# Routed rows that carry x with half of x1: the experts add it and scatter to the final place

## The chip, the core and the metric

The program runs on one core of a Trainium2 chip. The metric is the device time of one execution in microseconds, as the median of three runs: 1472.13 us before the change (1472.07 to 1477.34). Line numbers, as L1299, are those of the kernel before.

## What is computed

The input x has 4096 tokens of 128 numbers. Three blocks follow one another, each added to a running x:

```python
x = x + 0.5 * ffn(layernorm(x))       # first ffn
x = x + attn(layernorm(x))            # RWKV-6 recurrence
x = x + 0.5 * ffn(layernorm(x))       # second ffn, same weights

def ffn(z):
    x1 = z + msa(layernorm(z))        # softmax attention, 16 heads of 8, 512 tokens per batch
    return x1 + moe(layernorm(x1))    # one of 8 experts per token: gelu(h @ w1[e]) @ w2[e]
```

So each ffn block ends in x + 0.5 x1 + 0.5 y, where y is what the token's expert gives.

## The kernel before

The program is a chain of phases with a barrier of all engines between them: load_constants, mixer, expert, turn, recurrence, mixer, expert, combine. Each phase writes one instruction list per engine. The order on an engine is that of the code, and waits are on semaphores.

**Start.** In the first block SP issues 4 loads of constants, 8 slices of x (256 KB each) and 8 tables for the routing, and all engines wait for its end at a barrier (L259 to L282).

**Mixer.** It computes x1 in 8 batches b of 4 head groups g. Q and K are split in a high and a low part (`parts`: the high part by ScalarE, L866, the low part by VectorE, L979, or GpSimd, L518), and stored by SP to DRAM (`store`, L445), one image of 512 KB each per batch. From there SP loads each head group into stacked tiles `q_stack` and `k_stack` (`load_group`): 12 DMAs a group, 4 of 64 KB for q (L458) and 8 of 32 KB for k (L461), because both hold copies of the parts in several rows. TensorE makes scores (L652), VectorE their maxima (L986), TensorE the exponents' arguments (L660), ScalarE the exponentials (L933), TensorE the values (L670). `BEFORE`, `jobs` and `AFTER` are written lists that place the other work between these. Before the loop VectorE sets four stripes of `k_stack` to one (L1094) and then makes the low parts of batches 0 and 1. `halve` (L1022) makes x + 0.5 x1 in x_all, `norm_rows` (L1049) the normed x1 in `rows`, whose column 128 is the token's number. GpSimd scatters each row to its expert's place in the DRAM tensor `sorted` by indirect DMA (L558), 4 per batch. At the end SP writes 8 blocks of padding rows, one after each expert's rows, at places it reads from `pad_row` (L495, L496), and waits for them. GpSimd waits for all scatters.

**Expert.** 40 slots of 128 rows, as a software pipeline over three steps. In step j, SP has loaded tile j of `sorted` in one of 4 buffers `xt` (L1205), TensorE transposes it (L1228), ScalarE scales it (L1257), VectorE copies the expert's w1 (L1276); in step j+1 TensorE does the first layer (L1234), ScalarE the gelu (L1262); in step j+2 TensorE does the second layer (L1241), VectorE copies the result to `yt` (L1281). GpSimd casts the token numbers of a tile in the step after its transpose (L1295) and then scatters the rows of the tile before it to `expert_out` by indirect DMA (L1299). SP loads the next tile into a buffer once TensorE has transposed it and GpSimd has cast its numbers; the steps run in a loop unrolled by 4.

**Turn and combine.** The turn phase loads `expert_out` in 8 slices, VectorE adds half of it to x_all (L1400), norms it, TensorE transposes it for the recurrence. The combine phase at the end of the program loads it in 8 slices (L1317), adds half of it to x_all (L1323) and stores the output from ScalarE's queue (L1330).

**Phase exit.** All engines drain, GpSimd clears the phase's semaphores, and a barrier follows (L65, L66).

Of the kernel before, what the change touches and what calls it, by code (L numbers as in the profile page):

```python
# [5 lines left out]
F32 = mybir.dt.float32  # L6
# [7 lines left out]
P = 128  # L14
# [178 lines left out]
def load_constants(nc, ctx, d, x_all, padding, xs):  # L193
# [46 lines left out]

    def load_late(sp, part):
# [17 lines left out]
    with nc.Block() as block:  # L259
        @block.sync  # L260
        def _(sp):
            for dst, src in first:
                sp.dma_start(dst[:], src).then_inc(loaded, 16)
            for j in range(SL):
                here = slice(j * ST, (j + 1) * ST)
                sp.dma_start(x_all[:, here, :], x_slices[:, here, :]).then_inc(s["x_loaded"][j], 16)
            for dst, src in routing:
                sp.dma_start(dst[:], src).then_inc(s["routing_loaded"], 16)
# [10 lines left out]
        def _(pool):  # L279
            nc.gpsimd.memset(s["B_lora"][:], 0.0).then_inc(zeros_set, 1)  # L280
            nc.gpsimd.memset(padding[:, :, 0:P], 0.0).then_inc(zeros_set, 1)
            nc.gpsimd.memset(padding[:, :, P:], float(TOK)).then_inc(zeros_set, 1)  # L282
    return s, load_late, wait_rest


# [12 lines left out]
def mixer_phase(nc, ps, s, x_all, z_all, rows, expert, first_row, xs, qd, kd, load=None):  # L298
    with Phase(nc) as ctx:
# [71 lines left out]
        scattered, padded = sem("scattered"), sem("padded")  # L371
# [5 lines left out]
        PER_LOAD = 16 * 12  # L377
# [62 lines left out]
        with nc.Block() as block:  # L440
            @block.sync
            def _(sp):
                def store(j, k, dram):
                    sp.wait_ge(low[k], j + 1)
                    sp.dma_start(dram.rearrange("(c i) h t -> (i h) c t", i=DK)[:, :, j * SW:(j + 1) * SW],  # L445
                                 parts[k][:].bitcast(F32)).then_inc(stored[k], 16)

                def load_group(b, g):
                    def heads_of(dram, first, count, e):
                        heads = dram.rearrange("c (n p e) t -> c n p e t", p=PAIRS, e=2)  # L450
                        return heads[first:first + count, g, :, e, b * T:(b + 1) * T]

                    sp.wait_ge(stored["q"], 16 * (b + 1))
                    sp.wait_ge(stored["k"], 16 * (b + 1))
# [1618 lines left out]
```

## Time and profile before

The profile is of one execution that took 1473.18 us, of which 1471.4 us are the span from the first to the last instruction.

| what | us |
|---|---|
| median of the runs | 1472.13 |
| profiled execution | 1473.18 |
| its span | 1471.4 |
| first exponential of the first mixer | at 58.24 |
| first mixer to the start of the first expert phase | to 493.21 |
| first expert phase | 493.21 to 584.8 |
| turn phase | 585.3 to 610.2 |
| second mixer to the start of the second expert phase | 883.2 to 1362.74 |
| second expert phase | 1362.74 to 1453.5 |
| combine phase and end | 1453.5 to 1471.4 |

Starts are counted from the first instruction. The next phase begins only once the slowest engine has drained, so the end of a phase is set by the one wait that ends last there, and busy shares over the whole span say little about it.

### The profile page before, as it was taken

To read this page: it belongs to the slowest core of one execution; us is meant where nothing else is said; L and a number is where in the kernel's file an instruction comes from. 1 tells how busy PE (TensorE), PEld (TensorE's weight loads), DVE (VectorE), ACT (ScalarE), POOL (GpSimd) and SP (SyncE) were. 2 spreads that over 40 slices of the span, in tenths; PEclk is the share of its full clock that TensorE was granted. 3 is DMA by queue.
4 is the path that set the end of the run, shared out by engine and by line. 5 is a ranking of instruction groups with operands and counts; after the bars stand their busy time and mean duration, and the time that the engine had idled before them with its cause. 6 is when DMAs were issued, how large, how long until landed. Compare 5 with 4: busy or idle time off the path is not lost. (4 is left out here: it accounts for less than half of the span.)

```text
span 1471.4 us, 36051 instructions
## 1 busy us (share of the span) xinstructions
PE 1230.9 (84%) x12512; PEld 661.3 (45%) x12513; DVE 1042.9 (71%) x1842; ACT 860.7 (58%) x1742; POOL 553.6 (38%) x797
## 2 busy tenths in 40 slices
PE   2799999999997596398888754999999999993893
PEld 1234444444443596145455442344444444442893
DVE  3889988988992332478788745888898988963232
ACT  2288877778775353444334411588788778881451
POOL 6122324323212354355676536222332431222462
PEclk9599999999999799599999955799999999996896
DMA  4322442222110121100000003122122122100224
GB/s 117 71 74 74 130 121 68 82 71 73 55 36 9 53 67 47 42 2 3 3 2 2 3 1 87 57 75 65 49 82 73 53 81 66 56 15 30 56 66 122
DMA packets 81540, 82.40 MB, mean 56 GB/s; under 512 B 16249, under 2 KB 53724, under 8 KB 81392
## 3 DMA queue, kind: packets, MB, share of 16 engines
q1 hardware_dynamic: 72560, 69.88, 16.7%
q0 software_dynamic: 4608, 8.44, 1.8%
q10 hardware_dynamic: 4224, 2.10, 0.5%
q8 instruction: 94, 1.54, 0.4%
q14 instruction: 54, 0.44, 0.1%
HBM read 50.42 MB, written 29.93 MB: 55 GB/s over the span
## 5 line engine op out<-in xcount | busy, mean ns | idle before, releaser
L986 DVE TENSOR_REDUCE maxima<-ps 128x2 f32<-128x1024 f32 x512 | 616.2, 1222 | 89.8 <-PE ps L652 88.5
L933 ACT ACTIVATE probs<-ps 128x512 f32<-128x512 f32 x1024 | 550.8, 600 | 120.3 <-PE ps L660 109.7
L652 PE MATMUL ps<-k_stack,q_stack 62*128 62x512 f32 x1024 | 390.0, 473 | 39.0 <-DVE maxima L986 21.7
L660 PE MATMUL ps<-q_stack,k_stack 64*128 64x512 f32 x1024 | 396.3, 464 | 4.2 <-ACT q_whole L869 3.4
L670 PE MATMUL ps<-probs,v_stack 128*32 128x256 f32 x4096 | 329.6, 394 | 0.9 <-ACT probs L933 0.4
L652 PEld LDWEIGHTS ps<-k_stack,q_stack 62*128 62x128 f32 x1024 | 160.1, 194 | 235.9 <-issue 138.3
L660 PEld LDWEIGHTS ps<-q_stack,k_stack 64*128 64x128 f32 x1024 | 159.2, 187 | 30.5 <-ACT q_whole L869 8.6
L670 PEld LDWEIGHTS ps<-probs,v_stack 128*32 128x32 f32 x4096 | 81.7, 108 | 166.6 <-issue 148.3
L532 POOL CAST neg_wide<-maxima 128x16 fp32r<-128x16 f32 x64 | 12.6, 196 | 286.7 <-DVE maxima L986 286.7
L1299 POOL DMA_INDIRECT expert_out<-yt,number x80 | 78.3, 979 | 72.4 <-POOL number L1295 44.1
L1276 DVE COPY w_now<-w 128x512 f32 x80 | 34.6, 433 | 80.1 <-issue 42.2
L1234 PE MATMUL ps<-xT,w_now 128*128 128x128 f32 x640 | 89.7, 285 | 0.2
L1241 PE MATMUL ps<-w,hidT 128*128 x640 | 84.7, 276 | 0.0
L1234 PEld LDWEIGHTS ps<-xT,w_now 128*128 128x128 f32 x640 | 80.9, 198 | 3.0 <-issue 2.4
L1257 ACT ACTIVATE xT<-ps,ln_b,ln_w 128x128 f32<-128x128 f32 x80 | 36.6, 457 | 73.1 <-PE ps L1228 73.1
L1241 PEld LDWEIGHTS ps<-w,hidT 128*128 128x128 f32 x640 | 78.2, 193 | 0.1
L558 POOL DMA_INDIRECT sorted<-rows,slot x64 | 63.6, 994 | 37.8 <-issue 20.8
L542 POOL TENSOR_TENSOR rows<-o_rows,inv 128x128 f32<-128x128 f32 x64 | 30.8, 501 | 122.1 <-DVE inv L993 122.1
L1262 ACT ACTIVATE hidT<-ps 128x512 f32<-128x512 f32 x80 | 47.8, 597 | 40.3 <-PE ps L1234 39.8
L1731 POOL TENSOR_TENSOR r_kx<-r_kx,r_k_factor 128x512 f32<-128x512 f32 x48 | 61.6, 1284 | 9.8 <-PE ps L1909 6.4
L1712 POOL TENSOR_TENSOR r_mixed<-r_shift,zT 128x512 f32<-128x512 f32 x40 | 58.7, 1474 | 16.0 <-DVE r_shift L1588 16.0
L1281 DVE COPY yt<-ps 128x128 f32<-128x128 f32 x80 | 23.3, 291 | 48.8 <-PE ps L1241 48.1
(208 smaller groups left out, 1622.7 us busy)
## 6 DMA issues: line engine op xcount, KB each, us to landing
q_stack<-q_split SPq DMA_DIRECT2D x256, 64.0 KB
k_stack<-k_split SPq DMA_DIRECT2D x512, 32.0 KB
q_split<-q_parts SPq DMA_DIRECT2D x16, 512.0 KB, 2.7
k_split<-k_parts SPq DMA_DIRECT2D x16, 512.0 KB, 3.6
xt<-sorted SPq DMA_DIRECT2D x80, 64.5 KB
w<-in_L_ffn_w SPq DMA_DIRECT2D x16, 256.0 KB, 3.0
rows<-expert_out SPq DMA_DIRECT2D x16, 256.0 KB, 4.5
x_all<-in_L_attn_x SPq DMA_DIRECT2D x8, 256.0 KB, 5.1
```

The source lines that it names most:

```text
L558: pool.indirect_dma_start(xs, bass.IndirectOffsetOnAxis(ap=slot[:, i:i + 1], axis=0), rows[:, i, :], None).then_inc(scattered, 16)
L652: mm = t.matmul(psS[:, h, :], qs[g][score_rows(h), h // 2, u * P:(u + 1) * P], ks[g][score_rows(h), h // 2, :], start=True, stop=True)
L660: t.matmul(ring("e", G, u, n), ks[G % NG][half(h), h // 2, u * P:(u + 1) * P], qs[G % NG][half(h), h // 2, :], start=True, stop=True).then ...
L670: last = t.matmul(psO[VW * h:VW * (h + 1), here], vs[g][:, u, h, :], probs[u % 2][:, h, here], start=(g % SHARE == 0 and u == 0 and part = ...
L933: a.activation(probs[u % 2][:, h, :], ring("e", G, u, n), ACT.Exp, scale=float(DK) ** -0.5).then_inc(e_read, 1)
L986: v.tensor_reduce(maxima[G % 2][:, :, pair, u:u + 1], psS[:, 2 * pair:2 * pair + 2, :], AX_X, ALU.max, negate=True).then_inc(s_read, 1)
L1234: last = t.matmul(psH[o][:, c * P:(c + 1) * P], w1_now[o][:, c * P:(c + 1) * P], xT[o][:], start=True, stop=True)
L1241: last = t.matmul(psY[i][:, 0:P], hidT[i][:, c, :], s["w2"][:, ds(second_expert, 1), c, :], start=(c == 0), stop=(c == HC - 1))
L1262: a.activation(hidT[o][:].rearrange("p c t -> p (c t)"), psH[o], ACT.Gelu_apprx_tanh).then_inc(hidT_kept, 1)
L1299: pool.indirect_dma_start(ys, bass.IndirectOffsetOnAxis(ap=number[out_slot][:], axis=0), yt[out_slot][:], None, bounds_check=TOK - 1, oob_ ...
L1712: g.tensor_tensor(mixed[f][:], shift[f % 2][:], x, ALU.add).then_inc(mixed_ready.sem, 1)
L1731: g.tensor_tensor(dst[:].rearrange("p (k m) -> p k m", m=m), src[:].rearrange("p (k m) -> p k m", m=m), k_factor[l][:].rearrange("p n two ...
```

## The change

- `rows` becomes 257 numbers wide: normed x1, x_all, token number. x_all is now the middle part of `rows`, so a scattered row is 1028 bytes where it was 516. `sorted`, `padding` and `xt` are as wide.
- In the expert phase GpSimd copies the middle part of `xt` to a new tile `before` ahead of the cast of the numbers, SP's reload waits for it too, and VectorE's copy to `yt` becomes 0.5 y + `before`. The scatter goes to `after_experts` in the first ffn, and to the output in the second.
- The turn phase loads x_all itself and adds nothing. The combine phase goes.
- The first block loads 2 slices of x; the other 6 and the routing tables are issued by SP at the start of the mixer's block.
- The DRAM images of q and k have 32 rows, each part twice; each store is 2 DMAs of 512 KB, and a head group is loaded by 4 DMAs of 128 KB.
- VectorE makes the low parts of batch 0 ahead of the four memsets.
- Four padding blocks are written from SP's queue, four from ScalarE's.

```diff
@@ load_constants
+    def load_early(sp):
+        for j in range(2, SL):
+            here = slice(j * ST, (j + 1) * ST)
+            sp.dma_start(x_all[:, here, :], x_slices[:, here, :]).then_inc(s["x_loaded"][j], 16)
+        for dst, src in routing:
+            sp.dma_start(dst[:], src).then_inc(s["routing_loaded"], 16)
...
-            for j in range(SL):
+            for j in range(2):
                 here = slice(j * ST, (j + 1) * ST)
                 sp.dma_start(x_all[:, here, :], x_slices[:, here, :]).then_inc(s["x_loaded"][j], 16)
-            for dst, src in routing:
-                sp.dma_start(dst[:], src).then_inc(s["routing_loaded"], 16)
@@ mixer_phase
+                def store_k(j):
+                    sp.wait_ge(low["k"], j + 1)
+                    for a in range(SPLITS):
+                        every_other = kd.rearrange("(c a i) h t -> a c i h t", c=SPLITS, a=SPLITS)[a, :, :, :, j * SW:(j + 1) * SW]
+                        sp.dma_start(every_other.rearrange("c i h t -> (i h) c t"),
+                                     parts["k"][:].bitcast(F32)).then_inc(stored["k"], 16)
...
                     for e in range(2):
-                        for a in range(SPLITS):
-                            row = HALF * e + a * SPLITS * DK
-                            sp.dma_start(qs[g][row:row + SPLITS * DK, :, :].bitcast(F32),
-                                         heads_of(qd, 0, SPLITS * DK, e)).then_inc(loaded[g], 16)
-                            for at in (row, row + DK):
-                                sp.dma_start(ks[g][at:at + DK, :, :].bitcast(F32),
-                                             heads_of(kd, a * DK, DK, e)).then_inc(loaded[g], 16)
+                        here = slice(HALF * e, HALF * e + ROWS)
+                        sp.dma_start(qs[g][here, :, :].bitcast(F32), heads_of(qd, e)).then_inc(loaded[g], 16)
+                        sp.dma_start(ks[g][here, :, :].bitcast(F32), heads_of(kd, e)).then_inc(loaded[g], 16)
...
-                for e in range(E):
+                for e in range(E // 2):
                     row = sp.value_load(pad_row[0:1, e:e + 1], min_val=0, max_val=E * (TOK + P) - P)
                     sp.dma_start(xs[ds(row, P), :], s["padding"][:, 0, :]).then_inc(padded, 16)
...
+                act.wait_ge(pads_ready, 1)
+                for e in range(E // 2, E):
+                    row = act.value_load(pad_row[0:1, e:e + 1], min_val=0, max_val=E * (TOK + P) - P)
+                    act.dma_start(xs[ds(row, P), :], s["padding"][:, 0, :]).then_inc(act_padded, 16)
+                act.wait_ge(act_padded, 16 * (E - E // 2))
...
+                for k in "qk":
+                    low_part(0, k)
                 for i in range(2):
                     for e in range(2):
                         v.memset(ks[i][HALF * e + ROWS:HALF * e + STACK, :, :].bitcast(F32), 1.0).then_inc(k_set, 1)
-                for j in range(2):
-                    for k in "qk":
-                        low_part(j, k)
+                for k in "qk":
+                    low_part(1, k)
@@ expert_phase
                         sp.wait_ge(x_turned, RING * (turn - 1) + i + 1)
+                        sp.wait_ge(carried, RING * (turn - 1) + i + 1)
                         sp.wait_ge(numbered, RING * (turn - 1) + i + 1)
...
-                        v.tensor_copy(yt[out_slot][:], psY[i][:, 0:P]).then_inc(y_kept, 1)
+                        after(vec, carried, j, 2)
+                        v.scalar_tensor_tensor(yt[out_slot][:], psY[i][:, 0:P], 0.5, before[out_slot][:], ALU.mult,
+                                               ALU.add).then_inc(y_kept, 1)
...
-                        nc.gpsimd.tensor_copy(number[at][:], xt[at][:, P:]).then_inc(numbered, 1)
+                        nc.gpsimd.tensor_copy(before[at][:], xt[at][:, P:2 * P]).then_inc(carried, 1)
+                        nc.gpsimd.tensor_copy(number[at][:], xt[at][:, 2 * P:]).then_inc(numbered, 1)
@@ program
-        x_all, z_all = sb("x_all", [P, NT, P]), sb("z_all", [P, NT, P])
-        rows = sb("rows", [P, NT, P + 1])
+        z_all, rows = sb("z_all", [P, NT, P]), sb("rows", [P, NT, 2 * P + 1])
+        x_all = rows[:, :, P:2 * P]
...
-        ffn()
-        combine_phase(nc, x_all, y_all, ys, out)
+        ffn(out.rearrange("b t c -> (b t) c"))
```

## Rows read from the trace of the kernel before

**Rows 1.** The page of the profile: span, and busy time of each engine.
```profile
span 1471.4 us, 36051 instructions
...
PE 1230.9 (84%) x12512; PEld 661.3 (45%) x12513; DVE 1042.9 (71%) x1842; ACT 860.7 (58%) x1742; POOL 553.6 (38%) x797
```

**Rows 2.** Timeline of 0 to 14 us: start, length, engine, line, instruction [idle before].
```profile
2.58 5.73 SPq L266 DMA_DIRECT2D x_all<-in_L_attn_x  x8
...
13.01 0.87 DVE L950 BATCH_NORM_STATS2 stats<-x_all 128x6 f32<-128x128 f32 x4 [8.19 <-PEq L259]
```

**Rows 3.** Source view of line 266: from issue to landing.
```profile
DMA to landing us min/median/max: 3.1/5.1/5.9
```

**Rows 4.** Timeline of the second mixer's start, 893 to 908 us.
```profile
893.97 0.59 ACT L869 ACTIVATE k_whole<-ps 128x512 f32<-128x512 f32 x1
...
895.90 0.69 DVE L979 TENSOR_TENSOR k_parts<-k_whole,k_parts 128x512 fp32r<-128x512 f32 x1
...
900.64 0.33 SPq L458 DMA_DIRECT2D q_stack<-q_split  x1
...
907.30 1.22 PE L652 MATMUL ps<-k_stack,q_stack 62*128 62x512 f32 x4 [7.58 <-DMA k_stack<-k_split]
```

**Rows 5.** DMA view of 891 to 900 us in 40 equal slices.
```profile
GB/s 0 0 0 0 0 0 0 0 0 0 0 0 0 0 0 0 0 0 0 0 0 0 0 0 0 0 309 382 419 391 410 391 401 410 419 400 382 310 9 27
```

**Rows 6.** Timeline of the first mixer's end, 481 to 492 us.
```profile
481.32 8.46 SPq L496 DMA_DIRECT2D sorted<-padding  x8
...
484.83 0.96 POOL L558 DMA_INDIRECT sorted<-rows,slot  x1 [0.30 <-issue]
```

**Rows 7.** Source view of line 66 (phase exit) in windows at 491, 584, 1453 us.
```profile
L66 SPq DRAIN  x1: 7/7/7, 491.6 to 491.6; - x1
...
L66 SPq DRAIN  x1: 7/7/7, 584.8 to 584.8; - x1
...
L66 SPq DRAIN  x1: 7/7/7, 1453.5 to 1453.5; - x1
```

**Rows 8.** Timeline inside the first expert phase.
```profile
512.38 0.63 DVE L1276 COPY w_now<-w 128x512 f32 x1 [1.48 <-PE ps L1234]
...
512.75 0.29 POOL L1295 CAST number<-xt 128x1 int32<-128x1 f32 x1
...
540.88 0.29 DVE L1281 COPY yt<-ps 128x128 f32<-128x128 f32 x1 [0.62 <-PE ps L1241]
...
541.13 0.20 POOL L1295 CAST number<-xt 128x1 int32<-128x1 f32 x1
...
541.73 0.43 DVE L1276 COPY w_now<-w 128x512 f32 x1 [0.56 <-issue]
...
542.05 0.97 POOL L1299 DMA_INDIRECT expert_out<-yt,number  x1 [0.72 <-POOL number L1295]
...
544.51 0.14 PEld L1228 LDWEIGHTS ps<-ident,xt 128*128 128x128 f32 x1
...
577.55 0.97 POOL L1299 DMA_INDIRECT expert_out<-yt,number  x1 [0.61 <-issue]
```

**Rows 9.** Source views of lines 1205 (541.9 to 543.8 us) and 1299 (500 to 580 us).
```profile
L1205 SPq DMA_DIRECT2D xt<-sorted x1: 338/338/338, 542.3 to 542.3; - x1
...
L1299 POOL DMA_INDIRECT expert_out<-yt,number x40: 974/974/1154, 502.2 to 578.8; - x40
```

**Rows 10.** DMA issues on the page: KB each, median us from issue to landing.
```profile
w_qkv<-in_w_qkv SPq DMA_DIRECT2D x1, 192.0 KB, 2.3
...
ident<-in_ident SPq DMA_DIRECT2D x1, 64.0 KB, 1.9
```

**Rows 11.** Groups of instructions on POOL: count | busy us, mean ns | idle before.
```profile
L512 POOL TENSOR_SCALAR z_all<-x_all,moments,scales 128x128 f32<-128x128 f32 x64 | 50.5, 796 | 0.4
...
L524 POOL COPY v_stack<-v_all 128x144 f32<-128x144 f32 x64 | 20.0, 318 | 57.3 <-PE ps L670 57.0
```

**Rows 12.** Timeline of the turn phase, first add.
```profile
588.20 0.69 DVE L1400 SCALAR_TENSOR_TENSOR x_all<-rows,x_all 128x512 f32<-128x512 f32 x1 [10.49 <-DMA rows<-expert_out]
```

More of the change, by code:

```diff
@@ new lines, in store_q @@
+                def store_q(j):
+                    sp.wait_ge(low["q"], j + 1)
+                    for a in range(SPLITS):
+                        half_rows = qd[a * SPLITS * DK:(a + 1) * SPLITS * DK, :, j * SW:(j + 1) * SW]
+                        sp.dma_start(half_rows.rearrange("(c i) h t -> (i h) c t", i=DK),
+                                     parts["q"][:].bitcast(F32)).then_inc(stored["q"], 16)
+                def store_k(j):
+                    sp.wait_ge(low["k"], j + 1)
+                    for a in range(SPLITS):
+                        every_other = kd.rearrange("(c a i) h t -> a c i h t", c=SPLITS, a=SPLITS)[a, :, :, :, j * SW:(j + 1) * SW]
+                        sp.dma_start(every_other.rearrange("c i h t -> (i h) c t"),
+                                     parts["k"][:].bitcast(F32)).then_inc(stored["k"], 16)
@@ L469, in place @@
                                      max_rows[G % 2][e * count:(e + 1) * count, :].bitcast(F32)).then_inc(rows_placed, 16)
-                store(0, "q", qd)
-                store(0, "k", kd)
+                if load is not None:
+                    load[0](sp)
+                store_q(0)
+                store_k(0)
                 for g in range(NG):
                     load_group(0, g)
-                store(1, "q", qd)
-                store(1, "k", kd)
+                store_q(1)
+                store_k(1)
                 place(0)
@@ L482, in _ @@
                     if g == 3 and b + 2 < B:
[L483 to L484 removed]
+                        store_q(b + 2)
+                        store_k(b + 2)
                     if b + 1 < B:
@@ L555, in scatter @@
                     pool.wait_ge(row_ready, p + 1)
+                    pool.wait_ge(halved, p + 1)
                     pool.wait_ge(placed, p + 1)
@@ L894, in number @@
                     act.wait_ge(s["routing_loaded"], s["routing_count"])
-                    a.activation(rows[:, :, P:], s["token"][:].unsqueeze(2), ACT.Copy).then_inc(numbered, 1)
+                    a.activation(rows[:, :, 2 * P:], s["token"][:].unsqueeze(2), ACT.Copy).then_inc(numbered, 1)
                 def job(kind, j):
@@ L1195, in expert_phase @@
         number = [ctx.enter_context(nc.sbuf_tensor(own(nc, f"number{i}"), [P, 1], I32)) for i in range(RING)]
-        passed, numbered = sem("passed"), sem("numbered")
+        before = [ctx.enter_context(nc.sbuf_tensor(own(nc, f"before{i}"), [P, P], F32)) for i in range(RING)]
+        passed, numbered, carried = sem("passed"), sem("numbered"), sem("carried")
         second_done, y_kept, y_stored = sem("second_done"), sem("y_kept"), [sem(f"y_stored{i}") for i in range(RING)]
@@ L1304, in _ @@
                     pool.wait_ge(y_stored[i], 16 * (SLOTS // RING))
-def combine_phase(nc, x_all, y_all, ys, out):
-    with Phase(nc) as ctx:
-        y_loaded = [ctx.semaphore(f"y_loaded{j}") for j in range(SL)]
-        added, stored = ctx.semaphore("added"), ctx.semaphore("stored")
-        slices = [slice(j * ST, (j + 1) * ST) for j in range(SL)]
-        with nc.Block() as block:
-            @block.sync
-            def _(sp):
-                for j, here in enumerate(slices):
-                    sp.dma_start(y_all[:, here, :], tiles_of(ys)[:, here, :]).then_inc(y_loaded[j], 16)
-            @block.vector
-            def _(vec):
-                for j, here in enumerate(slices):
-                    vec.wait_ge(y_loaded[j], 16)
-                    nc.vector.scalar_tensor_tensor(x_all[:, here, :], y_all[:, here, :], 0.5, x_all[:, here, :],
-                                                   ALU.mult, ALU.add).then_inc(added, 1)
-            @block.scalar
-            def _(act):
-                for j, here in enumerate(slices):
-                    act.wait_ge(added, j + 1)
-                    act.dma_start(slices_of(out)[:, here, :], x_all[:, here, :]).then_inc(stored, 16)
-                act.wait_ge(stored, 16 * SL)
 class Signal:
@@ L1378, in turn_phase @@
         rstd, shift, normed = sbs("r_rstd", [P, ST]), sbs("r_shift", [P, ST]), sbs("r_normed", [P, ST, P])
-        y_loaded = [sem(f"y_loaded{j}") for j in range(SL)]
-        added, stats_made, moments_made, var_ready = sem("added"), sem("r_stats_made"), sem("r_moments_made"), sem("r_var_ready")
+        x_loaded = [sem(f"x_loaded{j}") for j in range(SL)]
+        stats_made, moments_made, var_ready = sem("r_stats_made"), sem("r_moments_made"), sem("r_var_ready")
         constants, rstd_ready, shift_ready = sem("r_constants"), sem("r_rstd_ready"), sem("r_shift_ready")
```

67 lines of the change are left out of this document (26 added, 41 removed).

## The prediction

> **What bounds the kernel now.** I read the page first. No engine is busy over the whole span [rows 1], so the stages have different limits, and the change touches their seams and the expert phases, hardly the attention in between. So I read the timelines at the seams, then one turn of the expert loop.
>
> Start: the first instruction that works on x, the statistics at 13.01, does not wait for its slice but for a block in which SP issues x for 5.73 us from 2.58, and the tables after it; VectorE, which had waited there for the four loads of constants, had been idle for 8.19 us [rows 2]. A mixer's start then hangs on q and k: low part of k, store, load, first scores at 907.30 with PE idle for 7.58 us on the load [rows 4]. A mixer's end hangs on SP: 8 padding blocks issue for 8.46 us from 481.32 while GpSimd has finished its scatters at 485.79 [rows 6], and SP drains at 491.6 [rows 7]. In the expert loop, PE paces: `yt` is followed 0.88 us later by the scatter (541.17 to 542.05), also where the number cast ended well before (577.55) [rows 8], so GpSimd waits for the result, not the result for GpSimd. The end is the combine phase, from the drain at 1453.5 to 1471.4 [rows 1, 7].
>
> **The change, part by part.** Span of the profiled execution 1471.4, its time 1473.18; the median is 1.05 below that time, and I take the same off at the end.
>
> *Later loads of x.* Two slices issue in 2 of 8 parts of 5.73 us, so SP is through at 4.0, VectorE at 13.01 - 8.19 = 4.8, and the barrier falls near 5. Slice 0 lands 3.1 us after its issue at best [rows 3], at 5.7. The statistics start at 5.7 instead of 13.01: **-7.3** (bounds: -8.0 if only the barrier counts, -5.3 with the median landing of 5.1). What SP issues now in the mixer's block is the rest, some 8.5 us, done by 14; the first low part comes at 25.1 - 7.3 = 18 or earlier, so it is not late. Slices 2 to 7 are used after 50 us. The wider padding memset ends before 4 us on GpSimd and is hidden.
>
> *Low parts ahead of the memsets.* k is whole at 894.56 and its low part ran only at 895.90, ending at 896.59 [rows 4]. It can now end at 895.3, 1.3 earlier, and q's about 1.7 before it. The memsets (about 4.7 us) end at 900 and the scores come after that, so nothing is late through them.
>
> *Images twice.* Before, 1 MB went out at some 400 GB/s in 2.6 us [rows 5], and SP began to load 4.05 us after the low part's end (900.64). Now 2 MB go out. q's megabyte goes first, k's starts when q's is out, at 897.2, and ends at 899.8; with the same tail the load begins at 900.6 to 900.9. The doubled store thus eats the 1.3 us. The load of the first group then issues 4 DMAs for 12. Before, 12 took about 4.2 us and the scores came 2.5 us after the last. Now 4 take 1.6, and 512 KB have to arrive in 4 DMAs instead of trickling: I take 904.8 for the first score, **-2.5** (bounds: 0 if the transfer and not the issue was the limit, -3.6 if neither the store nor the size costs anything). Twice, once per mixer: **-5.0**. Inside a mixer loads come a head group ahead of their use; I cost them and the extra 0.5 MB stores at nothing. If that cover failed, PE would show waits on `k_stack` DMAs outside the two starts; now it has them only there.
>
> *Padding on two queues.* Four blocks on SP end 4.2 us sooner, near 487.4. But then GpSimd is last: it ends its scatters at 485.79, and the landing of a last scatter can be read only at an expert phase's end, 578.8 + 0.97 to the drain at 584.8 [rows 7, 9], 5.0 us. So the drain falls at 490.8 instead of 491.6: **-0.8**, twice **-1.6** (bounds -3.6 each if a scatter lands in 2.2 us, as small plain DMAs do [rows 10]; +0.5 if the doubled row makes it later). The added wait on `halved` is met before `row_ready` in every batch, for halve stands before norm_rows; nobody queues behind it.
>
> *Expert phases.* GpSimd gains a copy of 128x128 per slot. The nearest row is the copy of 128x144 with 0.318 us, the farthest a tensor_scalar of 128x128 with 0.796 [rows 11]; same operation, so 0.30. The slot is (578.8 - 502.2)/39 = 1.96 us [rows 9]. GpSimd needs 0.97 + 0.20 + 0.30 and a gap between number and scatter, at most 0.61 where it was not the wait for `yt` alone [rows 8]: at most 2.08, likely 1.8. So it does not bind by itself. What binds is the ring of four `xt` buffers. The cast of tile j ends at 541.33, SP's reload of that buffer issues at 542.3 [rows 9], lands 1.9 later (64 KB [rows 10]) at 544.2 to 544.3, and PE wants it at 544.51 [rows 8]. Slack 0.2 us. The change adds 0.30 for the copy, 0.05 for the longer `yt` instruction (an estimate: one more operand), and 0.2 for 131 KB instead of 66 (192 KB land 0.4 later than 64 KB [rows 10], for twice this growth): 0.55 a turn of four slots. PE thus stalls 0.35 a turn, ten turns: 3.5 us a phase, **+7.0** (bounds 0 if the copy takes 0.15; see rivals for the top). The carried wait of SP is met before the numbered one; VectorE has slack of over a microsecond in a slot.
>
> One rule bears on this. By the Trainium skill, page SBUF — State Buffer, section "Who interferes with whom", VectorE in a two-port mode (copies between SBUF tiles can be in one) and GpSimd hold a shared port pair in turn, the later one blocked fully. The trace agrees where the two meet: a w1 copy of 0.63 over a cast of 0.29 at 512.38, where at 541 they are apart with 0.43 and 0.20 [rows 8].
>
> *Turn phase.* The first add of 0.69 goes [rows 12]; after it ScalarE paces the slices, so only this first one counts: **-0.7** (bounds 0 and -2).
>
> *No combine.* The last scatter goes straight to the output, with the same wait and drain at 1453.5. After that only the outer exit remains, about 1 us. 1471.4 - 1454.5 = **-16.9** (bounds -16 and -17.4).
>
> Sum: -7.3 - 5.0 - 1.6 + 7.0 - 0.7 - 16.9 = -24.5. 1473.2 - 24.5 = 1448.7, and on the level of the median **1448 us**.
>
> **The rivals.**
> - *GpSimd becomes the bound of the slot.* For: the gap after a cast is 0.72 at 542.05 [rows 8]. If it is needed in full, the slot is 0.97 + 0.20 + 0.30 + 0.72 = 2.19, +0.23 for 39 slots = 9 us a phase instead of 3.5: 1459. Against: the gap of 0.61 at 577.55.
> - *The copy meets the w1 copy.* Then it is late by up to 0.43 every turn, 4.3 us a phase more: 1456.5. Against: at 541.73 the w1 copy starts 0.4 us after the cast has ended, more than the 0.30 of the new copy [rows 8]. The skill's rule (the same page) would make this price the full one whenever they meet.
> - *Scatters land early.* Then the padding was the whole limit and each mixer ends 3.6 earlier, not 0.8: 1442. By the Trainium skill, page DMA: Bandwidth & Descriptors, section "Latency and other measured facts", a DMA's fixed cost is about 2 us, which would put it there. The 5.0 us at the expert's end speaks against it.
> - *Smaller ones.* Loading q and k is limited by the transfer: +5, 1453. A 1028-byte row costs GpSimd twice the time per scatter: four at each mixer end, +3.9 twice, 1456.
> - *Slower.* The GpSimd copy costs what the tensor_scalar costs and the gap of 0.72 stays. The slot becomes 0.97 + 0.20 + 0.80 + 0.72 = 2.69, +0.73 for 78 slots = +57 for +7: 1498. All else gives 31.5 back, 0.40 a slot, so it decides from a copy of about 0.47 us on. For: 0.796 is the same shape on the same engine. Against: it computes, the copy row does not.
>
> **How the numbers follow.** Forecast 0.50, GpSimd bound 0.14, port 0.08, early scatters 0.12, the smaller two 0.12, slower 0.04. The predicted time is the first's, 1448. The range takes in the early scatters with a ring that costs nothing (about 1437) and GpSimd as bound with a smaller start (about 1461). A measurement here tells 0.5%, 7.4 us, from no change; every case but the last is below 1464.8. Faster 0.93, same 0.03, slower 0.04.
>
> **What would show it.** Statistics at about 5.7; first score some 10 us earlier than before in the first mixer and 2.5 in the second; the first expert phase's slot at about 2.05 with PE waiting for `xt` once a turn, and GpSimd idle before the scatter for less than before; the drain of the mixer set by the last scatter, 5 us after its end; nothing after the last scatter but 6 us. Wrong would be: a slot that is GpSimd from end to end, PE waits on `k_stack` inside a mixer, a scatter on GpSimd over 1 us, or a w1 copy and the new copy always side by side.

## The result and the profile after

The kernel after takes 1458.91 us (median of 4 runs, 1456.21 to 1460.41), the kernel before 1473.35 beside it on the same chip: a ratio of 0.989, interval 0.9869 to 0.9911 (the two medians alone would give 0.990). By the medians that is 14.4 us faster, by the interval 13 to 19. The median lies inside the predicted range of 1437 to 1461, but 10.9 us above the predicted 1448. The profiled execution took 1458.89 us, with a span of 1456.9.

The page of the profile after, the lines that answer to [rows 1]:

```profile
span 1456.9 us, 35636 instructions
...
PE 1232.6 (85%) x12512; PEld 662.6 (45%) x12513; DVE 1033.9 (71%) x1826; ACT 860.6 (59%) x1742; POOL 573.1 (39%) x877
```

The totals say little, as before: PE is busy for 1.7 us more, GpSimd for 20, and the span is 14.5 us shorter. So I put the same moments of the two traces side by side. They are read from timelines and source views: first score, last cast of `slot` (the last thing before the last four scatters), and the moment at which the engines leave each phase's block.

| moment, us | before | after | the stretch before it changed by |
|---|---|---|---|
| first statistics | 13.0 | 5.6 | -7.4 |
| first score, mixer 1 | 37.2 | 27.0 | -2.8 |
| last `slot` cast, mixer 1 | 480.0 | 469.7 | -0.1 |
| mixer 1 left | 491.6 | 484.1 | **+2.8** |
| expert phase 1 left | 584.7 | 579.0 | +1.8 |
| turn phase left | 610.1 | 603.3 | -1.1 |
| statistics, mixer 2 (behind the recurrence) | 883.3 | 875.7 | -0.8 |
| first score, mixer 2 | 907.3 | 898.8 | -0.9 |
| last `slot` cast, mixer 2 | 1349.5 | 1343.4 | **+2.4** |
| mixer 2 left | 1361.1 | 1359.2 | **+4.2** |
| expert phase 2 left | 1453.4 | 1455.8 | +4.3 |
| end of the span | 1471.4 | 1456.9 | -16.9 |

The start, in the timeline of 0 to 8 us of the kernel after. VectorE waits 0.71 us for its slice of x where it had waited 8.19 for the block [rows 2]:

```profile
5.59 0.87 DVE L968 BATCH_NORM_STATS2 stats<-rows 128x6 f32<-128x128 f32 x4 [0.71 <-DMA rows<-in_L_attn_x]
```

The end, in the source view of line 66, 1450 to 1460 us. Two drains within 0.5 us, and then the span is over, where the combine phase stood before [rows 7]:

```profile
L66 SPq DRAIN  x2: 7/7/7, 1455.9 to 1456.4; - x2
```

**A mixer's end.** This is the seam that went the other way than predicted. First the source view of the block's line, 479 to 493 us, kernel before (an engine's COMPARE_BRANCH stands behind its last wait, its DRAIN behind that; the EVENT_SEMAPHORE is where all leave):

```profile
L440 POOLq COMPARE_BRANCH  x1: 43/43/43, 487.8 to 487.8; - x1
L440 POOLq DRAIN  x1: 2686/2686/2686, 488.0 to 488.0; - x1
L440 SPq COMPARE_BRANCH  x1: 43/43/43, 491.2 to 491.2; - x1
...
L440 SPq EVENT_SEMAPHORE  x1: 17/17/17, 491.6 to 491.6; - x1
```

And the same view of the kernel after, 475 to 486 us:

```profile
L446 ACTq COMPARE_BRANCH  x1: 43/43/43, 480.4 to 480.4; - x1
...
L446 POOLq COMPARE_BRANCH  x1: 43/43/43, 481.1 to 481.1; - x1
L446 POOLq DRAIN  x1: 2686/2686/2686, 481.3 to 481.3; - x1
L446 SPq COMPARE_BRANCH  x1: 43/43/43, 481.4 to 481.4; - x1
...
L446 SPq EVENT_SEMAPHORE  x1: 17/17/17, 484.1 to 484.1; - x1
```

(A landing is counted here from the end of the last scatter instruction on GpSimd to the moment at which the engine that waits for it passes its wait; a drain is the time of the DRAIN instruction behind that.) Before, GpSimd is through its wait for the scatters at 487.8, 2.0 us behind its last scatter (end 485.79), drains for 2.69 us and is ready at 490.7; SP's padding is through at 491.2 and decides, by half a microsecond. After, SP is through at 481.4, but GpSimd passes its wait at 481.1, 5.6 us behind its last scatter (end 475.52), and its drain then runs with nothing beside it: 484.0. In mixer 2 it is 7.0 us (1349.20 to 1356.2). So the scatters land late and GpSimd's drain is added to that. The DMA view of 478 to 494 us, kernel before (KB each, median us from issue to landing):

```profile
sorted<-padding SPq DMA_DIRECT2D x8, 64.5 KB, 2.0
```

and of 468 to 484 us, kernel after:

```profile
sorted<-padding ACTq DMA_DIRECT2D x4, 128.5 KB, 5.0
sorted<-padding SPq DMA_DIRECT2D x4, 128.5 KB, 5.4
```

Eight transfers on one queue, issued one in 1.06 us (8.46/8, [rows 6]), landed in 2.0 us each. Twice the bytes on two queues, beside four scatters of twice the bytes, land in 5.0 to 5.4.

**The expert phase.** The groups of PE and GpSimd in the kernel after, 1368 to 1450 us (count | busy us, mean ns | idle before):

```profile
L1249 PE MATMUL ps<-ident,xt 128*128 128x128 f32 x37 | 10.6, 285 | 3.3 <-DMA xt<-sorted 3.2
...
L1323 POOL DMA_INDIRECT out<-yt,number x40 | 39.2, 980 | 30.4 <-DVE yt L1303 17.8 <-issue 11.7 <-POOL number L1319 0.9
L1318 POOL COPY before<-xt 128x128 f32<-128x128 f32 x38 | 11.8, 311 | 0.0
```

The slot went from 1.96 us [rows 9] to (573.15 - 494.9)/39 = 2.01 in phase 1 and, from (1447.6 - 1372.2)/39 = 1.93 to (1450.0 - 1371.1)/39 = 2.02, in phase 2. PE, which had waited for no `xt` in this stretch, now waits 3.2 us for its loads. The copy costs 0.31 us, the scatter 0.98, as before. VectorE's `yt` now waits for the copy in some turns, 3.1 us in all in this window.

### The profile page after: what moved, and what is told of

It reads as the page before. It is cut to its first block and busy times, and to the rows that moved or that the text cites. A ratio compares the mean times of both kernels' runs of the same rounds, so it can differ in the third digit from the quotient of the medians.

```text
span 1456.9 us, 35636 instructions
## 1 busy us (share of the span) xinstructions
PE 1232.6 (85%) x12512; PEld 662.6 (45%) x12513; DVE 1033.9 (71%) x1826; ACT 860.6 (59%) x1742; POOL 573.1 (39%) x877
## 5 line engine op out<-in xcount | busy, mean ns | idle before, releaser
L544 POOL CAST neg_wide<-maxima 128x16 fp32r<-128x16 f32 x64 | 12.6, 196 | 283.0 <-DVE maxima L1004 283.0
L1303 DVE SCALAR_TENSOR_TENSOR yt<-ps,before 128x128 f32<-128x128 f32 x80 | 23.3, 291 | 57.2 <-PE ps L1262 50.6
L1249 PE MATMUL ps<-ident,xt 128*128 128x128 f32 x80 | 23.9, 298 | 46.7 <-DMA xt<-sorted 46.2
```

## The experiments

The times of whole kernels are medians of several runs, except where one run is named; moments inside a kernel are from its one trace. The runs were taken in four groups, each on a chip of its own with the kernel before beside it: 1472.91 us for `pads_one`, `before_pads_two`, `pads_after` and `ring8`; 1473.12 for the parts one at a time; 1472.23 for `sp_waits`, `best` and `best_two`; 1474.71 for `best_once`. What a kernel gains is therefore told against the before of its own group; the kernel after gained 14.4. The ratios' intervals are 1.5 to 7 us wide to either side, so a difference of 3 us between two changed kernels is settled by the traces, if at all, and not by the medians.

### Padding: one queue or two, beside the scatters or behind them

`pads_one`: the kernel after with all padding on SP again.

```diff
-                for e in range(E // 2):
+                for e in range(E):
...
-                act.wait_ge(pads_ready, 1)
-                for e in range(E // 2, E):
...
```

Expected:

> The changed kernel with all eight padding blocks back on SP's queue; everything else as changed. In the changed kernel the mixer ends 14.5 and 15.9 us after the last slot cast (before the change 11.6 and 11.7), and the last scatter lands 8.7 us after its end on GpSimd, with the DMA engines full for 8 us. Theory 'crowding': the eight padding blocks of 131 KB now leave in 4 us beside the scatters, and the last scatter waits in the crowd. Then with the blocks spread over 8.5 us the drain comes 11.6 to 12.5 us after the slot cast, and the kernel gains 4 to 6 us: about 1454. Rival 'long rows': a scatter of 1028-byte rows lands late by itself; the drain stays at 14.5 to 16 us and the time at 1459.

Measured: 1455.31 us, ratio 0.9871 (0.9848 to 0.9894), 17.6 us below its before, 3.2 more than the kernel after gained, with intervals that overlap. SP is through at 481.9 instead of 481.4, later; but GpSimd passes its wait at 479.7, 4.65 us behind its last scatter instead of 5.6, and the block is left 13.5 and 14.9 us behind the last cast instead of 14.4 and 15.8. That lies between the two theories: crowding had 11.6 to 12.5, long rows 14.5 to 16. The ends hold 1.8 of the 3.2 us, and in mixer 2 the end is again SP's padding (through at 1357.0, with GpSimd drained at 1355.2). The 8.7 us that the expectation called the landing is the landing and the drain together.

`before_pads_two`: the kernel before, only with the padding on two queues. Expected:

> The kernel before with only one part of the change: four padding blocks from SP's queue and four from ScalarE's, rows of 516 bytes. My forecast for this part was -0.8 us a mixer, since the last scatter would land 5.0 us after its end and set the drain: drain 10.8 us after the slot cast, time 1.6 us less. 'Crowding' with half the bytes: between that and no change (11.6). If scatters land in about 2 us when nothing is beside them, the drain comes 8 us after the slot cast and the time is 7 us less.

Measured: 1476.51 us, ratio 1.0025 (1.001 to 1.004): slower, where the prediction had taken 1.6 us off. The source view of the block's line, 479 to 494 us:

```profile
L440 ACTq COMPARE_BRANCH  x1: 38/38/38, 488.9 to 488.9; - x1
L440 SPq COMPARE_BRANCH  x1: 43/43/43, 489.1 to 489.1; - x1
...
L440 POOLq COMPARE_BRANCH  x1: 43/43/43, 489.3 to 489.3; - x1
L440 POOLq DRAIN  x1: 2686/2686/2686, 489.5 to 489.5; - x1
...
L440 SPq EVENT_SEMAPHORE  x1: 17/17/17, 492.3 to 492.3; - x1
```

The padding is done 2.1 us sooner than before, as meant (489.1 for 491.2). The scatters are through at 489.3 instead of 487.8, though their last one ended at the same moment (485.84 for 485.79), and with the 2.69 us of drain behind them the block is left at 492.3 instead of 491.6. With the short rows the second queue thus costs the scatters 1.5 us. Each mixer's end is 0.7 us longer, 1.4 together; of the 3.1 us by which this trace's span is longer, 2.2 lie inside mixer 2, in a stretch that is taken up in the section on the prediction.

`pads_after`: the kernel after, both padding queues waiting for all scatters first (one run).

```diff
                 sp.wait_ge(pads_ready, 1)
+                sp.wait_ge(scattered, 16 * NT)
...
                 act.wait_ge(pads_ready, 1)
+                act.wait_ge(scattered, 16 * NT)
```

Expected:

> The changed kernel with both queues of padding waiting until all scatters have landed; the time is not the point, the issue of the first padding block is, since it shows when the last scatter lands with nothing beside it. 'Crowding': first block issues 5.0 to 5.5 us after the last scatter's end, as at an expert phase's end. 'Long rows': 8 us or more after it. Time about 1465 in both.

Measured: 1461.06 us in its one run. GpSimd passes its wait 1.7 us behind its last scatter (475.27 to 477.0): without the padding beside them, even the 1028-byte rows land as fast as the short ones did beside 64 KB blocks. In mixer 2 it is 2.3. Both theories had more, 5.0 and 8. So a scatter's own landing is about 2 us, and the 5.0 us that the prediction had read at the expert phase's end is a landing and a drain. The trace of the kernel before has the two apart, in the source view of the expert block's line, 560 to 590 us: the last scatter ends at 579.8, GpSimd is through its wait 1.3 us later and then drains for 3.33.

```profile
L1200 POOLq COMPARE_BRANCH  x1: 38/38/38, 581.1 to 581.1; - x1
L1200 POOLq DRAIN  x1: 3325/3325/3325, 581.2 to 581.2; - x1
```

### GpSimd's drain

`sp_waits`: the kernel after, only with the waits for the last scatters on SP instead of GpSimd, in both phases.

```diff
                 sp.wait_ge(padded, 16 * (E // 2))
+                sp.wait_ge(scattered, 16 * NT)
...
                 scatter(B - 1)
-                pool.wait_ge(scattered, 16 * NT)
...
                         load(RING * turn + i, i)
+                for i in range(RING):
+                    sp.wait_ge(y_stored[i], 16 * (SLOTS // RING))
...
                 pipeline(pool, SLOTS, 2, step, unroll=RING)
-                for i in range(RING):
-                    pool.wait_ge(y_stored[i], 16 * (SLOTS // RING))
```

Expected:

> The kernel after, only with the waits for the last scatters moved from GpSimd to SyncE, in the mixer and in the expert phase. In the traces GpSimd's DRAIN at the end of a mixer takes 2.69 us in every kernel and 3.3 us at the end of the expert phase, and starts only when its wait for the scatters is over; all engines leave the phase when it ends. Theory: this drain in sequence sets the end; with the wait elsewhere it runs while the scatters and the padding land. Mixer end: 484.1 becomes about 481.8, the expert phase ends about 3 us earlier; 2 * 2.3 + 2 * 3 = 10 us, a median of about 1449. Rival: the drain's duration is the landing of the DMAs that GpSimd issued, so that it grows by what the wait no longer covers, and nothing is gained (1457 to 1460).

Measured: 1449.75 us, ratio 0.9828 (0.9785 to 0.9871): 22.5 us below its before, 8.0 more than the kernel after gained. The source view of the block's line, 468 to 483 us:

```profile
L446 POOLq DRAIN  x1: 10546/10546/10546, 471.1 to 471.1; - x1
...
L446 ACTq COMPARE_BRANCH  x1: 43/43/43, 479.7 to 479.7; - x1
...
L446 SPq COMPARE_BRANCH  x1: 41/41/41, 480.4 to 480.4; - x1
```

and of the expert block's line, 568 to 577 us:

```profile
L1220 POOLq DRAIN  x1: 4788/4788/4788, 571.0 to 571.0; - x1
```

Both theories had a part. The drain does run beside the landing now, but it is no fixed 2.69 us: it grew to 10.5 us and ends at 481.7, 1.3 us behind SP's last wait; in the expert phase it went from 3.33 us behind the wait to 4.79 in place of it. These two records start before the last scatters have run: behind the end of the last scatter (474.7 and 572.5) the drain lasts 7.0 and 3.3 us. From the last scatter's end to the leaving of the block: 8.6 and 10.0 us became 7.1 and 7.8 in the mixers, 4.9 became 3.5 in each expert phase. That is 1.5 + 2.2 + 1.4 + 1.4 = 6.5 us by the wait's place, not the 10 I had put down. The other 1.5 lie in stretches that the edit doesn't touch and that differ between executions by as much (the recurrence took 270.8 to 275.7 us in the fourteen traces).

### The ring of the expert phase

`ring8`: the kernel after with eight buffers instead of four.

```diff
-RING = 4
+RING = 8
```

Expected:

> The changed kernel with 8 instead of 4 buffers for xt, yt, before and number (and the step loop unrolled by 8). Theory 'ring': in the changed kernel the reload of a buffer reaches TensorE late once a turn; with eight buffers the waits for xt after the first tiles go, the slot falls from 2.01 and 2.02 us to 1.96 or less, and the kernel gains 3 to 5 us: about 1455. Rival 'GpSimd': its list of copy, cast and scatter paces the slot; the slot stays at 2.0 and the time at 1459.

Measured: 1449.74 us, ratio 0.9837 (0.9805 to 0.987): 23.2 us below its before, 8.7 more than the kernel after gained, and more than was expected. By the traces the ring holds 7.3 of it: the two expert phases are 2.3 and 5.0 us shorter than in the kernel after. Mixer 2 is also shorter, by 2.0 us at its start and 2.1 behind it, and other stretches are longer; the section on the prediction comes back to both. The same groups, 1368 to 1450 us:

```profile
L1249 PE MATMUL ps<-ident,xt 128*128 128x128 f32 x35 | 9.7, 277 | 0.0
...
L1323 POOL DMA_INDIRECT out<-yt,number x39 | 38.4, 985 | 18.8 <-issue 16.3 <-POOL number L1319 1.6 <-DVE yt L1303 1.0
L1318 POOL COPY before<-xt 128x128 f32<-128x128 f32 x38 | 11.8, 311 | 0.0
```

(The window also holds the end of the phase, which this kernel reaches earlier; the rates are in the slots.) PE waits for no load. The slot is 1.92 us in phase 1 and 1.89 in phase 2: below the kernel after by 0.09 and 0.13, and below the kernel before by 0.04 in both. The copy is still there and costs the slot nothing, and `yt` waits for no copy in this window. So four buffers may have been a small limit even before the change (that kernel wasn't run with eight); after it they are one.

### The parts one at a time, added to the kernel before

`before_x_later`, only the later loads of x:

```diff
-            for j in range(SL):
+            for j in range(2):
                 here = slice(j * ST, (j + 1) * ST)
                 sp.dma_start(x_all[:, here, :], x_slices[:, here, :]).then_inc(s["x_loaded"][j], 16)
-            for dst, src in routing:
-                sp.dma_start(dst[:], src).then_inc(s["routing_loaded"], 16)
...
+                if load is not None:
+                    load[0](sp)
```

> The kernel before, only with the later transfers of x and of the routing's constants put behind the first groups' work. The prediction's first term is -7.3 us. The trace after has the first statistics 7.42 us earlier, and if that gain is this part's alone and nothing gives it back, the median is 1472.9 - 7.4 = 1465.5. Rival: part of the gain is given back because x now lands among the stores and loads of the q and k images; then the first scores come less than 7.4 us earlier and the median is above 1467. Second rival: the whole mixer's start is set by something else that also changed, and this part alone gives under 3 us (above 1470).

Measured: 1465.72 us, ratio 0.9952 (0.9934 to 0.997): -7.4, by the interval -4 to -10, as the first theory has it; that it agrees to the tenth is luck. First score at 29.8, last cast at 472.4.

`before_images`, only the q and k images twice, with the changed functions `store_q`, `store_k` and `load_group`:

```diff
-                PER_LOAD = 16 * 12
+                PER_LOAD, STORED = 16 * 4, 16 * SPLITS
...
-                store(0, "q", qd)
-                store(0, "k", kd)
+                store_q(0)
+                store_k(0)
```

> The kernel before, only with the q and k images written twice into memory by the stores and each group's load made of 4 transfers of whole images instead of 12 parts. The order of the low parts stays. If this part is what brought the first scores of mixer 1 earlier by 2.8 us beyond the gain of x, the median falls by 2 to 5 us, to 1468 to 1471, with the first score at about 34.5 us. Rival: the order of the low parts on VectorE did it; then the first score stays at 37 us within 0.7 and the time within 1 us of before, and the next kernel shows the gain.

Measured: 1473.08 us, ratio 0.9995 (0.9981 to 1.001): nothing, as the rival has it. From the statistics to the first score it is 0.4 us less in mixer 1 (23.8) and 1.3 us more in mixer 2 (25.3).

`before_low`, only the order on VectorE:

```diff
+                for k in "qk":
+                    low_part(0, k)
                 for i in range(2):
...
-                for j in range(2):
-                    for k in "qk":
-                        low_part(j, k)
+                for k in "qk":
+                    low_part(1, k)
```

> The kernel before, only with the first low parts of q and k put ahead of VectorE's four memsets of the k images. If the order is what counts, the first score comes 1 us or more earlier in each mixer and the median is 1469 to 1471.5. If the images count, this is within 1 us of before (1472 to 1474) and the first score is at 36.6 to 37.2 us.

Measured: 1468.46 us, ratio 0.9971 (0.9961 to 0.9981): -4.7, a little more than the first theory had. First score 2.4 us earlier in mixer 1 (34.8) and 4.7 in mixer 2 (902.6), of which 2.8 lie between the statistics and the score.

`carry_alone`, only the wide rows, the sum in the expert phase and no last stage (the other parts undone; padding on SP):

> The kernel before, only with the routed rows carrying x and half of x1, the expert phase adding them and scattering to the tokens' rows, and no stage at the end; x early, the images once, the old order of the low parts, padding on one queue. The prediction's terms are +3.5 us per expert phase, -0.7 for the turn and -16.9 for the last stage: 1472.9 - 10.6 = 1462.3, with nothing for the longer rows that the mixer scatters. The rival, from the traces: the longer rows also cost at the end of each mixer, where the kernel after with one padding queue spends 13.6 and 15.0 us after the last slot instead of 11.6 and 11.7: 5.3 us more; with +1.7 and +4.3 us in the expert phases and -1.2 in the turn this makes 1472.9 - 16.9 + 5.3 + 6.0 - 1.2 = 1466.1.

Measured: 1462.95 us, ratio 0.9944 (0.9922 to 0.9965): -10.2 by the medians, -5 to -11.5 by the interval, which holds both the prediction's -10.6 and the rival's -6.8. The trace has the rival's mechanism, at half its price: the expert phases are 3.0 and 4.0 us longer, the turn 1.3 shorter, and the mixers' ends 1.0 and 1.5 longer, where the prediction had nothing. With -16.9 for the last stage that is -8.7; 2.4 us more come from the recurrence, which the edit doesn't touch. So the nearness to -10.6 is luck.

### The best of it

`best`: eight buffers, all padding on SP, SP waits for the scatters. `best_two`: the same, padding on two queues.

> The kernel after with eight buffers for the expert phase's tiles instead of four, all padding on SyncE, and the waits for the scatters on SyncE. Eight buffers alone gave 1449.7. With the padding on one queue SyncE's own 8 transfers land at 481.9, so the mixer's end gains little over one queue alone: 482.7 to 482.3, against 484.1 of the kernel after, 3 us for both mixers; the expert ends gain 3 us each if the drain theory holds: 1449.7 - 3.5 - 6 = 1440. If it doesn't: 1446.

> As the kernel before this one, but with the padding on two queues as in the kernel after. With GpSimd's drain out of the way the end is set by the last landing alone: the padding's last at 481.4 on two queues and 481.9 on one, the scatters at 481.1 and 479.7. So now two queues and one differ by under 1.5 us over both mixers, either way: 1439 to 1441. If two queues stay slower by 3 us as in the kernel after, then it isn't the drain that made them so.

Measured: `best` 1437.68 us (1437.17 to 1440.04), ratio 0.975 (0.9707 to 0.9794), the fastest kernel of this study. It is 34.5 us below its before, 20.1 more than the kernel after gained. `best_two` 1441.98 (1436.91 to 1442.64), ratio 0.9767 (0.972 to 0.9814). Their intervals overlap, and their mixers' ends are alike: 12.5 and 13.6 us behind the last cast with one queue, 12.8 and 13.9 with two. So with the waits on SP the second queue loses 0.3 us an end instead of 0.9, and gained nothing in any of the three arrangements that were tried. The ends are set differently from what was expected: with one queue SP's padding is last (480.9, GpSimd drained at 479.8), with two it is still GpSimd's drain (481.6, SP through at 480.4).

`best_once`: `best`, with the images written once and 12 loads a group.

> The best kernel so far (eight buffers, padding on SyncE alone, SyncE waits for the scatters), with the q and k images written once and loaded in 12 parts a group again, as before the change. The images alone moved nothing when added to the kernel before (1473.08 against 1473.12). Theory: they are worth nothing here either, and this is 1436.5 to 1439. Rival: they pay once VectorE's order of the low parts no longer hides them, since the first score waited for the k image's load again in the kernel after; then this is 1.5 to 4 us slower, 1439.5 to 1442.

Measured: 1442.33 us (1441.26 to 1443.78), ratio 0.9788 (0.9769 to 0.9808), 32.4 us below its before, where `best` was 34.5 below: the images are worth 2.2 us here. The two ratios' intervals overlap, so the runs alone don't settle it; the traces do. From the statistics to the first score it is 22.3 and 22.2 us with one image in the two mixers, 21.2 and 21.1 in `best`: 1.1 each, 2.2 together. So the rival holds, at its lower end: the images pay once the order on VectorE is the new one, though they paid nothing alone. The timeline of mixer 2's start, 862 to 892 us, kernel `best`:

```profile
879.20 0.69 DVE L992 TENSOR_TENSOR k_parts<-k_whole,k_parts 128x512 fp32r<-128x512 f32 x1 [1.01 <-ACT k_whole L882]
...
884.83 0.33 SPq L471 DMA_DIRECT2D q_stack<-q_split  x1
...
888.99 1.22 PE L665 MATMUL ps<-k_stack,q_stack 62*128 62x512 f32 x4 [4.79 <-DMA k_stack<-k_split]
```

and 865 to 897 us, kernel `best_once`:

```profile
882.64 0.69 DVE L988 TENSOR_TENSOR k_parts<-k_whole,k_parts 128x512 fp32r<-128x512 f32 x1 [1.01 <-ACT k_whole L878]
...
886.10 0.33 SPq L464 DMA_DIRECT2D q_stack<-q_split  x1
...
893.46 1.22 PE L661 MATMUL ps<-k_stack,q_stack 62*128 62x512 f32 x4 [5.95 <-DMA k_stack<-k_split]
```

The trade is in the open: from the low part's end to the first load 4.94 us with two images, 2.77 with one; from the first load to the first score 4.16 with two, 7.36 with one. +2.2 and -3.2.

## Why the prediction was right, and where it wasn't

It was right in sign and range. Of the 10.0 us that lie between the forecast for the span, -24.5, and the measured -14.5, one term holds most.

*The mixer's end is the term that failed.* The prediction took the padding on two queues at -0.8 a mixer, with bounds of -3.6 and +0.5; measured, +2.8 and +4.2, in sum 8.6 us off. Its picture was right in one thing, that GpSimd would be last. It failed in "the landing of a last scatter can be read only at an expert phase's end, ... 5.0 us". That 5.0 holds 1.3 us of landing and 3.33 of drain, was read where no padding moves, was taken as a landing alone, and was carried to a place where eight blocks of 128 KB go out at the same time. What the runs showed in its place: a landing of about 2 us without the padding (`pads_after`, 1.7 and 2.3), plus a drain of 2.69 us behind GpSimd's wait. The landing is stretched by the company: to 3.5 by two padding queues with the short rows, to 3.1 and 2.7 by the long rows on one queue (`carry_alone`), to 5.6 and 7.0 by both (after). `pads_one`, the long rows on one queue too, has 4.65 and 4.0: why more than `carry_alone` stays open. The longer rows at a mixer's end, a bound of +0.5 in the prediction, cost 1.0 and 1.5 us in `carry_alone`. The remedy of waiting elsewhere, `sp_waits`, is the test of the drain's part.

By the Trainium skill, page DMA: Bandwidth & Descriptors, section "Latency and other measured facts", a DMA's fixed cost is about 2 us; `pads_after` agrees with 1.7 and 2.3. The prediction had set this rule against the 5.0 of the trace and believed the 5.0 to be the same thing. The rival built on it, "scatters land early" (1442), had the landing right and the result wrong, since it left out both the drain and the company.

*Later loads of x*: -7.3 predicted, -7.4 measured, in the kernel after and alone.

*Low parts and images*: -2.5 a mixer predicted, -2.8 and -0.9 measured. The sum was near, its terms were not. The order on VectorE was put at 1.3 and is worth 2.3 to 2.8 (`before_low`): with q's low part ahead of the memsets, q's store is out before k's begins and k's lands sooner. In the timelines the time from the end of k's low part to the first load falls from 4.05 [rows 4] to 2.8 (893.15 to 895.93). The doubled store costs 2.2, not the 1.3 that was said, and the fewer loads give 3.2. In mixer 2 of the kernel after the load came 2.0 us later still than in `best` or in `ring8`, whose mixers are written alike (894.62 - 887.75 = 6.9 against 4.9). That is a wait for the k images to land. The traces show what it goes with: in this stretch of mixer 2 the DMA view lists one packet of a queue of kind "instruction", 0.02 MB, 0.4% of 16 engines over 15 us, so about 1 us of one engine. The four kernels with this mixer and four buffers (after, `pads_one`, `pads_after`, `sp_waits`) all have that packet and take 23.0 to 23.2 us from the statistics to the first score; the three with this mixer and eight buffers (`ring8`, `best`, `best_two`) don't have it and take 21.1 to 21.2. `before_images`, with 25.3, has it too. In mixer 1 none of them has it, and there the kernel after takes 21.4. So `ring8` owes 2.0 us of its gain to this start and not to the rate of its slots. That the packet causes the wait wasn't tested.

```profile
887.06 0.69 DVE L997 TENSOR_TENSOR k_parts<-k_whole,k_parts 128x512 fp32r<-128x512 f32 x1 [1.01 <-ACT k_whole L882]
...
894.62 0.33 SPq L471 DMA_DIRECT2D q_stack<-q_split  x1
...
898.85 1.22 PE L665 MATMUL ps<-k_stack,q_stack 62*128 62x512 f32 x4 [6.68 <-DMA k_stack<-k_split]
```

(Timeline of the kernel after, 885 to 900 us.) The DMA view of the same window (packets, MB, share of 16 engines):

```profile
q8 instruction: 1, 0.02, 0.4%
```

The loads inside the mixers were rightly put at nothing: between the two starts PE shows no wait for a `k_stack` DMA in the kernel after.

*The expert phases*: +3.5 each predicted, +1.8 and +4.3 measured, +3.0 and +4.0 in `carry_alone`. The mechanism, four buffers whose reload comes late, is shown by PE's waits and by `ring8`. Both rivals on the copy fail: GpSimd waits for `yt` (17.8 us) more than for anything else, the gap of 0.72 us before a scatter shrank to 0.3 to 0.5, and 0.31 us is what the nearest row had said. The 0.05 for a longer `yt` was wrong (0.29 us, as [rows 8]), and `ring8` suggests that the slack of 0.2 us was not there in every turn before the change either: its slot is shorter than that of before, with one copy more. The prediction's reading that its port rule agrees with the trace is weaker than it says: under the w1 copy of 0.63 us at 512.38 the timeline also has a scatter of GpSimd, from 511.78 to 512.75, so the cast alone wasn't shown to stretch it.

*The turn*: -0.7 predicted, -1.1 measured. *No combine*: -16.9 predicted, -16.9 measured.

*What was in no step*: mixer 2 takes 444.6 us from the first score to the last cast, where the kernel before has 442.2. This is not the change. The windows of 935 to 945 us, kernel before (busy us and count of PE, PEld, DVE, ACT, POOL, then the granted clock):

```profile
935.00:945.00 10.00, 9.61 (x87) 3.62 (x86) 9.37 (x19) 8.22 (x17) 3.80 (x6) 0.92 0.19 52
```

kernel `before_pads_two`, whose first score also comes at 907.3 and whose code is the same up to the padding:

```profile
935.00:945.00 10.00, 10.00 (x75) 3.49 (x74) 7.53 (x16) 6.56 (x14) 2.08 (x3) 0.70 0.11 28
```

TensorE was granted 0.50 in both while it waited between scores (915 to 935 us), that is 1.2 GHz, and came back to 1.00, 2.4 GHz, later in the second: 75 matmuls for 87. That kernel too needs 444.4 us for the stretch. Of the fourteen traces three have 444.4 to 444.6 there (the third is `sp_waits`), the others 441.8 to 442.6, whatever their code. Read in stretches of 5 us, the clock is back at 1.00 some 33.6 us behind the first score in exactly these three, and 27.3 to 32.3 us behind it in the other eleven, and the stretch grows with that delay, within 0.1 us: 441.8 us at 27.3, 442.2 at 29.3 (before), 442.5 at 32.0, 444.4 to 444.6 at 33.6. So the stretch goes with the late clock. Why the last 1.3 us of delay go with 1.8 us and the 5 us before them with 0.8 is not shown, and no run set the clock's return by itself.

The parts alone make -7.4 + 0.0 - 4.7 - 10.2 = -22.3 with the padding on one queue. The kernel after with one queue, `pads_one`, stands at -17.6 to the kernel before of its group. The four parts' intervals and that of `pads_one` together are about 6 us wide to either side, so the missing 4.7 may be noise in part. In the traces, the mixers' ends hold 0.9 and 1.8 (13.5 and 14.9 us behind the last cast, against 12.6 and 13.1 in `carry_alone`), and the start of mixer 2 holds 1.9 (23.1 us from the statistics to the first score, against 21.2 in `before_low`), the stall above.

## What to carry to other kernels

A phase ends with the last of several engines, and two that stand half a microsecond apart have to be costed together: here the one that was relieved was the visible one, and the one behind it was made later by the relief. A transfer's landing belongs to the traffic that it was read in; before carrying it to another place, take apart what is landing and what is the engine's drain behind its wait, and ask what else goes out at that moment. And where a reload of a buffer has a slack of 0.2 us, more buffers (here eight for four) can be worth more than the instruction that threatens it.

## What the runs showed of the hardware that was not expected

- GpSimd's drain at the end of a block in which it has issued indirect DMAs took 2.69 us in the mixer and 3.33 us in the expert phase, behind a wait for the very same DMAs; in the turn phase, where it issues none, 0.30. Without that wait it took 10.5 and 4.8 us, from before the last scatters had run, 7.0 and 3.3 of it behind the last one's end, and ended about 1.3 us (mixer) and 2.1 us (expert) behind the last scatter's landing as SP saw it.
- Splitting eight stores over two queues made each land in 3.9 to 4.1 us instead of 2.0 (64.5 KB, the kernel before), and delayed indirect DMAs of a third queue by 1.5 us.
- An indirect DMA of 128 rows took 0.96 us of GpSimd with rows of 516 and of 1028 bytes alike.
- Two stores of 512 KB each, to two images, in place of one, landed in 3.6 us (q) and 5.3 us (k) instead of 2.7 and 3.6, by the page's medians.
